# Biased attention: queries and keys projected three pairs ahead, output weights split at the end of the stage before

## The reference, cut to what matters

```python
q = h @ wq; k = h @ wk; v = h @ wv            # h: 8 x 256 x 256, weights 256 x 1024, 16 heads of 64
scores = q @ k.T + bias[head, j - i]          # bias from a table by relative position, no scale
out = softmax(scores) @ v                     # 8 batches x 16 heads x 256 x 256
x = layernorm(h + out @ wo)                   # wo 1024 x 256
```

## Time and profile before

| | |
|---|---|
| median of 3 runs | 2071.15 us (2067.23 to 2071.71) |
| profiled execution: time | 2052.55 us |
| profiled execution: span | 2050.3 us |
| busy PE / DVE / ACT / POOL | 86% / 56% / 49% / 36% |
| biased attention, first load to last output | 893 to 1327 us of the span |
| granted TensorE clock, mean | 0.929 of full speed |

### The profile page before, as it was taken

The page is one execution under the profiler, slowest core; times in us unless marked ns, Lnnn a source line. Parts: engine busy times, 40 slices in busy tenths (PEclk is TensorE's granted clock), DMA queues, the critical chain, the costliest instruction groups (busy, mean ns, idle before and its releaser), DMA issues. The chain is left out here.

```text
span 2050.3 us, 40780 instructions
## 1 busy us (share of the span) xinstructions
PE 1764.3 (86%) x15132; PEld 1417.3 (69%) x15132; DVE 1142.2 (56%) x3109; ACT 1007.6 (49%) x2377; POOL 741.0 (36%) x653
## 2 busy tenths in 40 slices
PE   7988885789849999959999999588889995999994
PEld 5777664676628989847777777466567774788883
DVE  3666664456445555535555555545558772457774
ACT  4555551345325454535555555245546662356663
POOL 2334332667332424113333333321234442434443
PEclk9999996799759999989999999989969997999997
DMA  2000002000063444330000000011100406623334
GB/s 69 12 12 12 22 6 81 1 12 27 17 214 102 118 130 113 104 87 2 11 12 12 12 12 7 22 51 55 32 18 18 150 25 223 229 81 51 52 52 103
DMA packets 93673, 121.25 MB, mean 59 GB/s; under 512 B 8458, under 2 KB 80602, under 8 KB 93450
## 3 DMA queue, kind: packets, MB, share of 16 engines
q1 hardware_dynamic: 80186, 100.89, 15.0%
q0 software_dynamic: 13296, 17.77, 5.0%
HBM read 82.94 MB, written 37.80 MB: 59 GB/s over the span
## 5 line engine op out<-in xcount | busy, mean ns | idle before, releaser
L2021 POOL TENSOR_TENSOR L1a_probs<-L1a_probs,L1a_rinv 128x1024 f32<-128x1024 f32 x64 | 121.2, 1894 | 261.6 <-DVE L1a_rinv L2345 261.6
L2018 POOL TENSOR_TENSOR L0a_probs<-L0a_probs,L0a_rinv 128x256 f32<-128x256 f32 (+1 forms) x128 | 103.1, 826 | 190.3 <-DVE L0a_rinv L2345 190.3
L2337 DVE CUSTOM_DVE_ANT_0 L1a_sbias<-L1a_psS,L1a_bias 128x256 f32<-128x256 f32 x256 | 93.2, 421 | 100.1 <-PE L1a_psS L2132 100.0
L2286 ACT ACTIVATE L1a_probs<-L1a_sbias,L1a_nmx 128x256 f32<-128x256 f32 x256 | 126.5, 497 | 44.2 <-DVE L1a_nmx L2337 44.2
L3017 POOL DMA_INDIRECT moe_sums<-moe_y,moe_xg x39 | 83.5, 2141 | 134.8 <-DVE moe_y L3316 125.7
L2619 POOL DMA_INDIRECT ec_sums<-ec_yk,ec_token_at x32 | 61.0, 1905 | 189.9 <-ACT ec_yk L2744 184.7
L2286 ACT ACTIVATE L0a_probs<-L0a_sbias,L0a_nmx 128x128 f32<-128x128 f32 (+1 forms) x256 | 112.8, 443 | 28.8 <-DVE L0a_nmx L2337 28.8
L2803 DVE TENSOR_TENSOR ec_h<-ec_sg,ec_psU 128x512 f32<-128x512 f32 x64 | 44.0, 687 | 119.9 <-ACT ec_sg L2727 119.9
L2046 PE MATMUL L1a_psF<-L1a_xT,ec_wt 128*128 128x256 f32 x720 | 101.3, 291 | 9.4 <-DVE L1a_xT L2362 8.5
L2046 PEld LDWEIGHTS L1a_psF<-L1a_xT,ec_wt 128*128 128x128 f32 x720 | 89.0, 191 | 24.2 <-DVE L1a_xT L2362 11.7
L3095 PE MATMUL moe_psY<-moe_wts,moe_hT 128*128 (+1 forms) x440 | 104.0, 379 | 0.8 <-ACT moe_hT L3162 0.8
(11 more groups left out here) (593 smaller groups left out, 4934.8 us busy)
## 6 DMA issues: line engine op xcount, KB each, us to landing
shelf<-in_L_ffn_w_gate SPq DMA_DIRECT2D x8, 1024.0 KB, 9.2
shelf<-in_L_ffn_w_up SPq DMA_DIRECT2D x8, 1024.0 KB, 13.0
ec_wd<-in_L_ffn_w_down SPq DMA_DIRECT2D x8, 1024.0 KB, 6.2
moe_rows<-blank SPq DMA_DIRECT2D x1, 5070.0 KB, 19.2
moe_xg<-moe_rows SPq DMA_DIRECT2D x39, 130.0 KB, 2.1
moe_wts<-in_L_ffn_e_gate SPq DMA_DIRECT2D x8, 512.0 KB, 10.1
moe_wts<-in_L_ffn_e_up SPq DMA_DIRECT2D x8, 512.0 KB, 9.9
moe_wts<-in_L_ffn_e_down SPq DMA_DIRECT2D x8, 512.0 KB, 10.0
```

Source lines behind the costliest of these rows:

```text
L2018: last = pool.tensor_tensor(v, v, bcast(rinv[:, r, :, t], 2, KEYS[t]), ALU.mult)
L2021: last = pool.tensor_tensor(v, v, bcast(rinv[:, r, :, :].rearrange("p h t -> p (h t)"), 2, S), ALU.mult)
L2286: ins = act.activation(probs[:, r, j, at], sbias[:, g % 2, j, at], ACT.Exp, bias=nmx[:, r, j, t:t + 1], scale=-1.0, accum_out=sums[:, r, j ...
L2337: last = dve.tensor_tensor_reduce(out=sbias[:, g % 2, j, at], in0=psS[:, slot + j, at], in1=added, scale=-1.0, scalar=LARGE, op0=ALU.add, ...
```

## The change

- Queries and keys of pair p + 3 are projected in half 0 of step p, for the same batch as long as p + 3 < 8, else for the next (before: all of the next batch, spread over halves). The front has only qk 0 to 2 and three v items; v(1, 1) follows in step 0 of its own batch. xT of the next batch moves from step 0 to step 4, v(0, 0), v(1, 0), v(0, 1) of the next batch to steps 5 to 7, out stays in step 1.
- The bias turns are spread otherwise over the shorter front. A v item in the front waits for the take of the item directly before it.
- The input of batch b + 1 is normalized in pairs 1 and 2 of batch b; only batch 0 is normalized in the front.
- wo is split at the end of the expert choice: ACT's copy after its last scaled copy, DVE's subtraction after those of v. `lower_out`, its semaphore and its waits are gone.
- Queries and keys get a buffer of their own; the shelf ends with the expert choice, and the experts' split down weights (`wdt`) live on as wo.

```diff
-            qk = stage
+            qk = sb("qk", [P, 2, NP, 2, S])
...
-            TURNS = [(), (), (0, 1), (2, 3), (4, 5, 6), (7, 8, 9), (10, 11, 12), (13, 14, 15)]
-            FRONT = (("xT",), *(("qk", p) for p in range(NP)), ("v", 0, 0), ("v", 1, 0), ("v", 0, 1), ("v", 1, 1))
-            PLAN = {(0, 1): ("xT",), (1, 0): ("qk", 0), (1, 1): ("out",), (2, 1): ("qk", 1),
-                    (3, 0): ("qk", 2), (3, 1): ("v", 0, 0), (4, 0): ("v", 1, 0), (4, 1): ("qk", 3), (5, 0): ("qk", 4),
-                    (5, 1): ("qk", 5), (6, 0): ("qk", 6), (6, 1): ("qk", 7), (7, 0): ("v", 0, 1), (7, 1): ("v", 1, 1)}
+            TURNS = {("qk", 1): (0, 1, 2, 3), ("qk", 2): (4, 5), ("v", 0, 0): (6, 7, 8, 9), ("v", 1, 0): (10, 11, 12),
+                     ("v", 0, 1): (13, 14, 15)}
+            FRONT = (("xT",), ("qk", 0), ("qk", 1), ("qk", 2), ("v", 0, 0), ("v", 1, 0), ("v", 0, 1))
+            PLAN = {(0, 1): ("v", 1, 1), (1, 1): ("out",), (4, 1): ("xT",), (5, 1): ("v", 0, 0), (6, 1): ("v", 1, 0),
+                    (7, 1): ("v", 0, 1)}
+            for p in range(NP):
+                PLAN[p, 0] = ("qk", (p + 3) % NP)
...
-                if not latent and g in (1, 2):
-                    lower_out(g - 1)
-                if not latent and g % NP == 6 and g // NP + 2 < B:
-                    root_input(g // NP + 2)
+                if not latent and g % NP == 1 and g // NP + 1 < B:
+                    root_input(g // NP + 1)
...
-                elif not latent and 2 <= n < len(FRONT):
+                elif not latent and 2 <= n < len(FRONT) and what[0] != "v":
                     pe.wait_ge(item_taken, n - 1)
...
-                if not latent and n == 4:
-                    split(wo[:, 0, :, :].rearrange("p a b -> p (a b)"), raw_o)
...
-                if not latent and p == 7 and b + 2 < B:
-                    apply_input(b + 2)
+                if not latent and p == 2 and b + 1 < B:
+                    apply_input(b + 1)
...
-                if not latent and b + 2 < B:
-                    if p == 6:
-                        input_stats(b + 2)
-                    elif p == 7:
-                        input_shift(b + 2)
+                if not latent and b + 1 < B:
+                    if p == 1:
+                        input_stats(b + 1)
+                    elif p == 2:
+                        input_shift(b + 1)
...
+                act.wait_ge(next_in[3], 16)
+                act.activation(wdt[:, 0, :, :], next_o(), ACT.Copy).then_inc(next_high, 1)
...
+                dve.wait_ge(next_high, 4)
+                dve.tensor_tensor(wdt[:, 1, :, :], next_o(), wdt[:, 0, :, :], ALU.subtract).then_inc(next_low, 1)
```

More of the change, by code:

```diff
@@ L1833, in wide_stage @@
         if not latent:
-            shelf_life, split_life, shelf, wqk, wv, sums_in = held
+            split_life, wqk, wv, wo, sums_in = held
             ctx.callback(split_life.close)
             x_in = sums_in.rearrange("(b t p) d -> b p t d", t=TT, p=P)
-            ctx.callback(shelf_life.close)
         sem = Semaphores(nc, name)
@@ L1848, in wide_stage @@
         oT = sb("oT", [P, 2, NP, S], F32R)
-        wo = sb("wo", [P, 2, NP, D], F32R)
+        if latent:
+            wo = sb("wo", [P, 2, NP, D], F32R)
         y = sb("y", [P, TT, D])
@@ L1872, in wide_stage @@
         else:
-            stage = shelf[:].rearrange("p (z n j s) -> p z n j s", z=2, n=NP, j=2)
-            raw_o = stage[:, 1, 4:8, :, :].rearrange("p a b c -> p (a b c)")
-            qk = stage
+            qk = sb("qk", [P, 2, NP, 2, S])
             wqkv = {"q": wqk[:, :, 0, :, :], "k": wqk[:, :, 1, :, :], "v": wv}
@@ L1903, in wide_stage @@
         w_ready = sem("w_ready")
-        o_lowered = sem("o_lowered")
         in_step, in_asked, in_rooted, in_shifted, x_normed = (sem("in_" + k) for k in ("step", "asked", "rooted", "shifted", "normed"))
@@ L1923, in wide_stage, with batch_of @@
         else:
-            TURNS = [(), (), (0, 1), (2, 3), (4, 5, 6), (7, 8, 9), (10, 11, 12), (13, 14, 15)]
-            FRONT = (("xT",), *(("qk", p) for p in range(NP)), ("v", 0, 0), ("v", 1, 0), ("v", 0, 1), ("v", 1, 1))
-            PLAN = {(0, 1): ("xT",), (1, 0): ("qk", 0), (1, 1): ("out",), (2, 1): ("qk", 1),
-                    (3, 0): ("qk", 2), (3, 1): ("v", 0, 0), (4, 0): ("v", 1, 0), (4, 1): ("qk", 3), (5, 0): ("qk", 4),
-                    (5, 1): ("qk", 5), (6, 0): ("qk", 6), (6, 1): ("qk", 7), (7, 0): ("v", 0, 1), (7, 1): ("v", 1, 1)}
+            TURNS = {("qk", 1): (0, 1, 2, 3), ("qk", 2): (4, 5), ("v", 0, 0): (6, 7, 8, 9), ("v", 1, 0): (10, 11, 12),
[5 more added lines that the diff above has]
+                PLAN[p, 0] = ("qk", (p + 3) % NP)
+        def batch_of(p, half, b):
+            what = PLAN[p, half]
+            if what[0] == "out":
+                return b - 1
+            if not latent and (half == 0 and p + 3 < NP or what == ("v", 1, 1)):
+                return b
+            return b + 1
         ORDER = [(f, 0) for f in FRONT]
@@ L1932, in wide_stage @@
             for (p, half), what in sorted(PLAN.items()):
-                at = b - 1 if what[0] == "out" else b + 1
+                at = batch_of(p, half, b)
                 if 0 <= at < B:
@@ L2003, in _ @@
                 root_input(0)
[L2004 to L2010, removed]
             def normalize(g):
@@ L2105, in item @@
                         pe.wait_ge(w_ready, 9)
-                    else:
-                        pe.wait_ge(o_lowered, 2)
                     for t in range(TT):
@@ L2196, in _ @@
                 item(what, 0)
-                if what[0] == "qk":
-                    for h in TURNS[what[1]]:
+                if not latent:
+                    for h in TURNS.get(what, ()):
                         turn_bias(h)
@@ L2234, in take @@
                 elif what[0] == "qk":
-                    if b == 1 and what[1] == NP // 2:
-                        act.wait_ge(o_lowered, 2)
                     ins = act.activation(qk[:, b % 2, what[1], :, :].rearrange("p a s -> p (a s)"), ps, ACT.Copy)
@@ L2275, in _ @@
                 take(("xT",), 0)
-                apply_input(1)
             def exponential(g):
@@ L2428, in _ @@
                 input_shift(0)
-                input_stats(1)
                 take(("xT",), 0)
-                input_shift(1)
             if not latent:
@@ L2489, in expert_choice_run @@
     x_rows = x_in.rearrange("b p t d -> b t p d").rearrange("b t p d -> (b t p) d")
-    shelf_life = ExitStack()
-    shelf = shelf_life.enter_context(nc.sbuf_tensor("shelf", [P, 2 * 2 * KD * I], F32))
     with ExitStack() as ctx:
+        shelf = ctx.enter_context(nc.sbuf_tensor("shelf", [P, 2 * 2 * KD * I], F32))
         def sb(n, shape, dt=F32):
@@ L2501, in expert_choice_run @@
         wt = split_life.enter_context(nc.sbuf_tensor("ec_wt", [P, 2, 2, KD, I], F32R, side="right"))
+        wdt = split_life.enter_context(nc.sbuf_tensor("ec_wdt", [P, 2, IC, D], F32R, side="right"))
         next_v = split_life.enter_context(nc.sbuf_tensor("next_v", [P, 2, KD, I], F32R, side="right"))
@@ L2521, in expert_choice_run @@
         hT = sb("hT", [P, 2, IC, SL], F32R)
-        wdt = sb("wdt", [P, 2, IC, D], F32R)
         yk = sb("yk", [P, 2, ST, D])
@@ L2555, in next_parts, with next_o @@
             return wt[:, z, 0, :, :], wt[:, z, 1, :, :], next_v[:, z, :, :]
+        def next_o():
+            return shelf[:, 3 * KD * I:4 * KD * I].rearrange("p (c k) -> p c k", c=IC)
         def next_raw(n):
@@ L2815, in _ @@
                             dve.tensor_tensor(low, next_raw(n), high, ALU.subtract).then_inc(next_low, 1)
-    return shelf_life, split_life, shelf, wt, next_v, sums
+                dve.wait_ge(next_high, 4)
+                dve.tensor_tensor(wdt[:, 1, :, :], next_o(), wdt[:, 0, :, :], ALU.subtract).then_inc(next_low, 1)
+    return split_life, wt, next_v, wdt, sums
 def moe_stage(nc, consts, x_in, base_in, x_out, a):
```

## The result

The changed kernel takes 2057.06 us (median of 7 runs, 2047.37 to 2061.1), the kernel before, run beside it, 2069.79 (2065.02 to 2076.9): a ratio of 0.992, 95% interval 0.9895 to 0.9946, or 12.7 us less. The biased attention, first load to last output, went from 433.0 to 417.6 us, and its first load came 0.9 to 1.0 later behind the last scaled copy of the expert choice (12.3 instead of 11.3). Together about -14.4.

A forecast was written before the change was run, and what follows sets the result against it. PE was taken to bound the front and middle batches, while the last batch has room. The terms -12.95 - 4.9 + 2.6 + 1.7 = -13.55 us took 2071.15 to 2057.6 us; range 2050 to 2066 us.

The forecast's parts named there:

- front, to scores(2): Start of the biased attention: with fewer qk and v items, scores(2) starts at 925.9 instead of 935.70 us.
- front and batch 0 together: From the attention's start to the next batch: that batch starts at 967.8 instead of 980.75 us, -12.95 us.
- six middle batches: Same PE work otherwise spread over the steps: 48.7 instead of 49.52 us each, together -4.9 us.
- last batch: Qk and v items enter steps with idle PE time: 29.3 instead of 26.72 us, +2.6 us.
- scatter: End of the expert choice: DVE's subtraction delays the fourth scatter (+1.1) or the third too (+2.3); taken as +1.7 us.
- The forecast's case: Whole kernel: items moved into steps with idle PE time are nearly free; 2052 to 2061 us, chance 0.60.
- (a): Rival: middle batches gain nothing, as steps 4 and 5 or ACT's apply eat 0.8; -8.65 us, 2062.5, chance 0.22.
- (b): Rival: each item costs its full 1.6 in the last batch, the middle gains nothing; -1.65 us, 2069.5, chance 0.07.
- (c): Rival: ACT's take of qk comes one exponential (2.0 us) late and scores slip; +8.65 us, 2079.8, chance 0.05.
- (d): Rival: part of the front's gain fails (bias copies, late takes); in all between -10 and -4 us, chance 0.06.
- The step that had to hold: Single-item steps: ACT's take of qk ends at 3.35, scores ask at 4.3, so 0.95 us is to spare.
- the loop through `out_low`: Steps without items: scores, row maxima, reciprocal, out_low, then values; it ends PE's idle time, 1.52 us in the last batch.

The follow-up runs named there:

- e1: Kernel before with only the new order of projections, bias turns and input normalization, output weights split as before: 2055.29 us, ratio 0.9909.
- second profile: Changed kernel, unedited, run again on another chip beside the better version: 2034.85 us, ratio 0.9939.
- e3: Changed kernel with the qk items of steps 2 and 3 moved to half 1, behind ACT's exponential: 2070.91 us, ratio 0.9999.
- e6: Kernel before with DVE's out_low put ahead of the row maxima in the biased attention: 2056.42 us in one run.
- e4: Changed kernel with DVE's subtraction at the end of the expert choice made three times: 2061.9 us in one run.
- e7: Changed kernel with ACT's take of xT ahead of its step's exponential and the seam's subtraction in eight pieces: 2031.98 us, ratio 0.9892.
- e9: Changed kernel with xT taken ahead of the exponential and the subtraction in eight pieces, beside the unedited changed kernel: 2026.13 us, ratio 0.9894.
- e2: Changed kernel with the old order of projections, only the output weights split at the end of the expert choice: 2072.04 us, ratio 0.9995.
- e5: Kernel before, unedited, profiled a second time on another chip: 2054.8 us, median there 2053.05.

## Why the prediction was right, step by step
| term | predicted | measured |
|---|---|---|
| front, to scores(2) (part of the next row) | -9.8 | -8.35 (34.0 against 42.35) |
| front and batch 0 together | -12.95 | -11.74 |
| six middle batches | -4.9 (48.7) | -6.9 (48.37) |
| last batch | +2.6 (29.3) | +2.5 (29.26) |
| behind the last scores | 0 | +0.8 |
| scatter | +1.7 | +0.9 |
| sum | -13.55 | -14.4 |

Against -12.7 by the medians. The forecast's case held; (a), (b), (c) and (d) did not occur, the misses are of size. They partly cancel in the sum (+1.2, -2.0, +0.8, -0.8), and the base came out 1.4 lower than assumed while the gain by medians is 0.8 smaller: that 2057.06 lies so near 2057.6 is in part luck.

- **Front.** I took a qk item at 1.6. Item 1 took 2.76 (899.72), at a granted clock of 0.50, the lower of the two levels (1.2 GHz); before it took 1.67, at a mean of 0.92. In both kernels it starts 11.4 to 11.5 after the first load with 3.8 busy us of PE before it. The later rise goes with the moved weights in all seven profiles that have them (see e1), by a way that no run shows; the prediction put the front's share of that edit at 0. By starts it is 0.96 of the 1.45 missed; item 1 starts 0.14 later, and four turns at 3.05 instead of 2.8 are 0.25 more. Scores(2) at 34.0, and at 33.35 in the second profile, missed the 32 to 33 that I had named as a sign. The first normalization, no longer covered by v items, costs 0.19 before the first turn. Batch 0 behind it came to 41.66; I had 41.9.
- **Middle.** All eight steps stand within 0.11 of the layout: 6.00, 10.30, 4.28, 4.29, 5.00, 6.50, 6.00, 6.00. Most of the 0.33 is in step 1 (10.30, not 10.41) and in step 5, where the wait for xT is 0.43 and not 0.6. The step that had to hold was that ACT's take of qk is over before the next scores; it was, 0.94 ahead of them (987.75 against 988.69), and e3 shows what it is worth. In rival (c) I counted eight steps 4 with xT; there are seven, which makes it 0.3 less.
- **Last batch.** Right to 0.1: an item that came alone to its step cost 0.1 to 0.2 (steps 1 to 4), not 1.6. Step 0, which got two, went from 4.16 to 6.0: the second costs its full length, so the six together cost 2.5 and not 9.6. e6 adds what I had not seen: behind the loop through `out_low` POOL's normalization stands only 0.1 to 0.2 away. That loop bounds the empty steps as well, so my case rests on room for PE, not on one waiting instruction. The +0.8 behind the last scores is values of 1.97 at the lower clock behind the hole of 1.52; that stretch is 22.4 to 22.5 in e1, e4, e7 and e9 too (e3: 23.2), but 21.7 in the second profile of the changed kernel, as in before, e2 and e5. So the term comes with the new order, though not in every execution.
- **Scatter.** The mechanism was right (end of the subtraction plus 1.43), and the fourth scatter alone was right to 0.2: +1.1 laid out, +0.9 measured. The term was mis-sized since I took the middle between that and +2.3, a third scatter held as well; it was free. (Laid out like the first, a held third comes to +2.9: 888.1 + 0.3 + 1.55 against 887.1.) By the rule of the Trainium skill (SBUF — State Buffer, "SBUF: two separate sides"), that the two exclude each other for whole instructions, the subtraction would have waited for the third scatter until 879.16 and held the fourth to 1.43 after 881.45, an estimate of +1.9. It began at 878.22, inside the third, so here row and rule part, and the measurement decides.
- **The base.** I took over 18.6 us between profiled execution and median. That held only because I added the sum to the median: the changed kernel's profiled execution (2055.67) lies 1.4 under its median. The gap fits the form of the last stage, 23.0 us between its two forms. Had I forecast the profiled span (2036.8), I would have missed by 17. Before's profiled time of 2052.55 lies below all seven of its timed runs beside the changed kernel (2065.02 to 2076.9) and within those of e5's chip (2050.03 to 2056.09), so it is most likely of another chip or session than they. How often each form occurs within the timed runs, no profile shows.

What stays open: why the last stage has two forms. It is bound to neither kernel; its waits are named only as another core or an unknown queue. Open too is why the granted clock rises later in the front once the weights are split a stage earlier.

## What to carry to other kernels
Look for steps in which the busiest engine waits for a loop elsewhere, and move work there from stretches where it has no holes: the same work was worth 1.6 an item in one place and 0.1 to 0.2 in the other, as long as only one was added to a step. When look-ahead is shortened, write down at which moment of the step the product is taken and at which it is asked for: here 0.94 us of slack carried the gain, and two items behind an exponential lost all of it. Before comparing two single profiles, compare the stages that the change does not touch; here one of them differed by more than the whole change.

## What the runs showed of the hardware that I had not expected
- POOL's scatter and a DVE subtraction of 128x2048: the scatter that starts inside it ends 1.43 after it, in before, in the changed kernel and in e4 alike (3.45 or 2.47 long), the one already running is neither lengthened nor does it hold the subtraction back, and later subtractions don't lengthen it (e4). In eight pieces the subtraction takes 2.77 instead of 2.29 and the scatter 1.61. The other way round, a small DVE instruction stood 1.52 instead of 0.17 until POOL's subtraction ended (e1).
- With the output weights split at the seam, the granted clock rose 12.9 to 15.0 us after the attention's first load in seven profiles of seven, without it at 11.5 to 11.7 in four of four. The cause is open.
- A hole of 1.94 us in PE, made by a gain of 1.0, was followed by 2.9 us at half the granted clock; the one of 0.72 in the same place was not.
- The last stage of the same program takes 23 us more or less from one chip or session to another, at equal durations of its instructions on POOL.
